# Expert outputs added to rows in device memory as they are made, and a last stage whose down product comes a group later

## The reference

```python
shared = silu(xf @ sg) * (xf @ su) @ sd
masked = expert scores, -1e9 outside the best 4 of 8 groups
top_scores, top_idx = top_k(masked, 4)        # 4 of 32 experts for each token
gates = softmax(top_scores)
pos = place of the token in its expert's list; keep = pos < 1280
buf[e, pos] = xf[token]                       # kept tokens
out_e = (silu(buf @ wg) * (buf @ wu)) @ wd    # 32 experts, hidden 512
contrib = out_e[e, min(pos, 1279)] * gate * keep
out = layernorm(xf + shared + sum of the 4 contribs)
```

## Time and profile before

| | |
|---|---|
| median of 3 timed runs | 2529.51 us |
| profiled execution, time | 2515.5 us |
| its span, first to last instruction | 2514.0 us |
| mean granted TensorE clock | 0.949 |
| PE busy | 2225.7 us, 89% |
| DVE, ACT, POOL busy | 59%, 43%, 51% |
| indirect transfers | 256 scatters, 240 gathers, 256 row fetches |
| moved by DMA | 271.14 MB |

### The profile page before, as it was taken

How to read it: one execution, slowest core, us unless ns; L and a number is a source line. 1 busy time by engine, 2 the same in 40 slices (tenths; PEclk the granted TensorE clock), 3 DMA queues, 4 the chain that set the end, 5 groups by cost and what they waited for, 6 DMA issues and landing times. The chain is left out here.

```text
span 2514.0 us, 45293 instructions
## 1 busy us (share of the span) xinstructions
PE 2225.7 (89%) x12892; PEld 1786.8 (71%) x12892; DVE 1490.4 (59%) x3485; ACT 1076.3 (43%) x2818; POOL 1292.9 (51%) x1564
## 2 busy tenths in 40 slices
PE   6999699999999999506999999999999994887885
PEld 3555366666666666406999999999999994776774
DVE  4666246666666766524555556565655552767766
ACT  3555254454544445204555555555555551222221
POOL 3666211565565564654444444444444444677775
PEclk9999799999999999758999999999999997998997
DMA  4000122233142131104554444444444453344443
GB/s 129 25 0 0 46 77 91 60 78 99 59 98 77 59 117 52 62 1 155 151 154 151 153 158 159 155 155 159 159 159 159 157 154 106 117 130 129 138 127 102
DMA packets 196419, 271.14 MB, mean 108 GB/s; under 512 B 30745, under 2 KB 139057, under 8 KB 196370
## 3 DMA queue, kind: packets, MB, share of 16 engines
q1 hardware_dynamic: 164370, 209.30, 26.4%
q0 software_dynamic: 32000, 61.26, 9.1%
HBM read 182.75 MB, written 87.73 MB: 108 GB/s over the span
## 5 line engine op out<-in xcount | busy, mean ns | idle before, releaser
L1351 POOL DMA_INDIRECT e_xg<-x_rows,e_tok x240 | 243.8, 1016 | 443.2 <-issue 229.2
L967 POOL DMA_INDIRECT slot_token<-tok,a_slot_i x256 | 267.9, 1046 | 214.3 <-issue 95.7
L1636 POOL DMA_INDIRECT f_row<-expert_rows,f_idx x256 | 265.8, 1038 | 89.9 <-issue 76.7
L1479 ACT ACTIVATE e_sg<-e_g 128x448 f32<-128x448 f32 x232 | 126.5, 545 | 420.1 <-PE e_g L1205 420.1
L1529 DVE TENSOR_TENSOR e_hid<-e_sg,e_u 128x448 f32<-128x448 f32 x232 | 144.1, 621 | 246.7 <-PE e_u L1205 242.7
L850 ACT ACTIVATE a_prob<-a_s,a_ntop 128x128 f32<-128x128 f32 x512 | 180.1, 394 | 0.8 <-DVE a_ntop L1147 0.5
L1542 DVE COPY e_out<-e_d 112x512 f32<-112x512 f32 x116 | 80.2, 691 | 150.9 <-PE e_d L1205 150.9
L1205 PE MATMUL e_d<-e_wd1h,e_ht1h 128*112 128x256 f32 x464 | 132.9, 286 | 13.3 <-issue 13.3
L1205 PE MATMUL f_d<-f_wdh,f_hth 128*128 128x256 f32 x256 | 83.0, 324 | 60.3 <-DVE f_htl L1756 60.3
L1727 ACT ACTIVATE f_sg<-f_g 128x512 f32<-128x512 f32 x64 | 38.2, 598 | 224.6 <-PE f_g L1205 224.6
L1205 PE MATMUL e_d<-e_wd0h,e_ht0h 128*112 128x256 f32 x464 | 132.0, 285 | 0.0
(11 more groups left out here) (262 smaller groups left out, 6630.2 us busy)
## 6 DMA issues: line engine op xcount, KB each, us to landing
expert_rows<-a_zero SPq DMA_DIRECT2D x16, 2688.0 KB, 12.6
e_raw_g<-in_eg SPq DMA_DIRECT2D x60, 512.0 KB, 3.4
e_raw_u<-in_eu SPq DMA_DIRECT2D x60, 512.0 KB, 4.4
e_raw_d<-in_ed SPq DMA_DIRECT2D x59, 512.0 KB, 5.9
expert_rows<-e_out SPq DMA_DIRECT2D x58, 448.0 KB, 3.1
x<-in_x SPq DMA_DIRECT2D x16, 512.0 KB, 3.6
x_rows<-x SPq DMA_DIRECT2D x16, 512.0 KB, 3.5
f_xs<-x_rows SPq DMA_DIRECT2D x16, 512.0 KB, 4.9
```

The costliest lines, as they stand in the source:

```text
L967: pool.indirect_dma_start(k.slot_tok, bass.IndirectOffsetOnAxis(ap=slot_i[:, j, q:q + 1], axis=0), k.tok[:, j:j + 1], None, bounds_check=S ...
L1351: pool.indirect_dma_start(xg[a][:, n, :], None, k.x2_d, bass.IndirectOffsetOnAxis(ap=tok[a][:, n:n + 1], axis=0))\
L1479: act.activation(sg[m % 2][:], bank_g[m % 2][:, 0:SETW], ACT.Silu).then_inc(sg_rdy, 1)
L1636: pool.indirect_dma_start(row[a][:, j, q, :], None, k.out_d[0:SLOTS, :], bass.IndirectOffsetOnAxis(ap=idx[a][:, j, q:q + 1], axis=0))\
```

## The change

- Gates and token numbers are scattered together as pairs of 8 bytes. `slot_token` gets two columns; blank slots name rows behind the real ones. The two on-chip tables, and the vector instructions that fill them, are gone, and `place` waits for the scatters of the group before at the gates, five instructions earlier. The zero fill of `expert_rows` is gone; x2 is stored twice, to `x_rows` and to `sum_rows`, in which the sums grow.
- In the expert stage VectorE multiplies the down product by the gates, four instructions for the two copies. GpSimd adds the 448 rows to `sum_rows` by four indirect transfers that add (`add_rows`), two items later. Two items can hold the same token, so the adds of an item wait for those of the item before to land; the wait passes over SyncE, whose `load_dest(w)` (the pairs once more, for the gates and the addresses) waits for the adds of item w-2.
- In the last stage the row fetches and the sixteen adds are gone. SyncE loads x2 for the transposes and the sums for the last addition separately. TensorE makes `down(g-1)` after `turn(g+1)`; the hidden parts have two buffers. VectorE's `summed`, `moments` and `normed` come up to a group later; GpSimd has only `rstd`.
- The plan's last column holds the number of items less one, from which the ends of the loops are worked out; the rounds are the same.

```diff
-                FILLED = SLOTS // NG
-
-                sp.wait_ge(blank_rdy, 1)
-                sp.dma_start(k.slot_tok.rearrange("(p n) a -> p (n a)", p=RT), blank[:]).then_inc(blanked, 16)
+                spare = zero[0:RT, None, :].to_broadcast([RT, TI, D])
+                sp.wait_ge(blank_rdy, 2)
+                sp.dma_start(k.slot_tok.rearrange("(p m n) a -> p m (n a)", p=BLANKS, n=SETW),
+                             blank[:].rearrange("p n a -> p (n a)")[:, None, :]
+                             .to_broadcast([BLANKS, (E * NSET + 1) // BLANKS, 2 * SETW])).then_inc(blanked, 16)
                 sp.wait_ge(zero_rdy, 1)
+                for d in (k.x2_d, k.acc_d):
+                    sp.dma_start(d[B * T:B * T + SETW, :].rearrange("(p n) d -> p n d", n=TI), spare).then_inc(filled, 16)
 
                 def store(g):
-                    sp.dma_start(k.out_d[bass.ds(g * FILLED, FILLED), :].rearrange("(p n) d -> p n d", p=P),
-                                 zero[:, None, :].to_broadcast([P, FILLED // P, D])).then_inc(filled, 16)
                     sp.wait_ge(x2_rdy, ONE + g + 1)
-                    sp.dma_start(k.x2_d[bass.ds(g * GW, GW), :].rearrange("(b t) d -> t b d", b=TG),
-                                 grouped(rows(k.x, g))).then_inc(x2_out, 16)
+                    for d in (k.x2_d, k.acc_d):
+                        sp.dma_start(d[bass.ds(g * GW, GW), :].rearrange("(b t) d -> t b d", b=TG),
+                                     grouped(rows(k.x, g))).then_inc(x2_out, 16)
...
-                                k.tok[:, j:j + 1], None, bounds_check=SLOTS - 1, oob_is_err=False)\
+                                pair[:, j, q, :], None, bounds_check=SLOTS - 1, oob_is_err=False)\
...
+                    dve.wait_ge(tok_rdy, ONE + r)
+                    then(dve.tensor_tensor(pair_gate, ex[:], er[:, :, None].to_broadcast([P, TG, K]), ALU.mult))
...
-                def store(w, a):
+                def load_dest(w, a):
                     start = slots(w)
-                    sp.wait_ge(out_rdy, OUT + NP * (w + 1))
-                    sp.dma_start(k.out_d[bass.ds(start, SETW), :].rearrange("(p n) d -> p n d", n=TI), out[a][:])\
-                        .then_inc(stored[a], 16)
+                    if at_least(w, 2):
+                        sp.wait_ge(added, 16 * TI * (w - 1))
+                        apart(sp, k.past_sp)
+                    sp.dma_start(dest[a][:], k.slot_tok[bass.ds(start, SETW), :].rearrange("(p n) a -> p n a", n=TI))\
+                        .then_inc(dest_in[a], 16)
 
                 def item(w, a):
                     load_tok(w + 2, a)
                     load_up(w + 2, a)
                     load_down(w + 1, 1 - a)
-                    if at_least(w, 1):
-                        store(w - 1, 1 - a)
+                    load_dest(w, a)
...
+                def add_rows(w, a):
+                    pool.wait_ge(out_rdy, OUT + TI * (w + 1))
+                    apart(pool, k.past_pool)
+                    for n in range(TI):
+                        pool.indirect_dma_start(k.acc_d, bass.IndirectOffsetOnAxis(ap=dest[a][:, n, 0:1], axis=0),
+                                                out[a][:, n, :], None, compute_op=ALU.add).then_inc(added, 16)
+
+                def item(w, a, i):
+
+
+                    gather(w + 2, a, i + 1)
+                    if at_least(w, 2):
+                        pool.wait_ge(u_done, ONE + HC * w + 2)
+                        apart(pool, k.past_pool)
+                        pool.wait_ge(dest_in[1 - a], DMA + 16 * (i + a))
+                        apart(pool, k.past_pool)
+                        add_rows(w - 2, a)
+                    down_low(w, a)
...
+                pool.wait_ge(dest_in[1], DMA + 16 * used)
+                apart(pool, k.past_pool)
+                add_rows(last - 1, 0)
+                pool.wait_ge(added, 16 * TI * last)
+                apart(pool, k.past_pool)
+                add_rows(last, 1)
...
-                def copied(w, a, i):
-                    if at_least(i, 1):
-                        dve.wait_ge(stored[a], DMA + 16 * i)
-                    for h in range(NP):
-                        dve.wait_ge(d_done, ONE + NP * w + h + 1)
-                        dve.tensor_copy(out[a][:, 2 * h:2 * h + 2, :],
-                                        bank_d[h][0:RT, :].rearrange("p (t d) -> p t d", t=2)).then_inc(out_rdy, 1)
+                def gated(w, a, i):
+
+                    dve.wait_ge(dest_in[a], DMA + 16 * (i + 1))
+                    gate = dest[a][:].bitcast(F32)
+                    for n in range(TI):
+                        if n % 2 == 0:
+                            dve.wait_ge(d_done, ONE + NP * w + n // 2 + 1)
+                        dve.tensor_scalar(out[a][:, n, :], bank_d[n // 2][0:RT, (n % 2) * D:(n % 2 + 1) * D],
+                                          gate[:, n, 1:2], None, ALU.mult).then_inc(out_rdy, 1)
...
+                def fetch_acc(g, a):
+                    sp.dma_start(acc[a][:], acc_rows[:, bass.ds(g * TG, TG), :]).then_inc(acc_in[a], 16)
...
+                        sp.wait_ge(t_done, ONE + DC * (g + 1))
+                        apart(sp, k.past_sp)
+                        fetch(g + 2, a)
                         sp.wait_ge(sum_rdy, ONE + 2 * (g + 1))
                         apart(sp, k.past_sp)
-                        fetch(g + 2, a)
+                        fetch_acc(g + 2, a)
                         store(g, a)
...
-                    if not first:
-                        pool.wait_ge(row_in[a], 16 * TG * K * i)
-                    pool.tensor_copy(idx[a][:].rearrange("p t q -> p (t q)"),
-                                     k.slot[:, bass.ds(g * TG * K, TG * K)]).then_inc(idx_rdy, 1)
-                    pool.wait_ge(idx_rdy, ONE + g + 1)
-                    apart(pool, k.past_pool)
-                    for j in range(TG):
-                        for q in range(K):
-                            pool.indirect_dma_start(row[a][:, j, q, :], None, k.out_d[0:SLOTS, :],
-                                                    bass.IndirectOffsetOnAxis(ap=idx[a][:, j, q:q + 1], axis=0))\
-                                .then_inc(row_in[a], 16)
+                begin(pool, ve_rdy, rs_rdy)
 
...
+                def group(g, a, i):
+                    up(g)
+                    if not is_last(g):
+                        turn(g + 1, 1 - a, i + a)
+                    if at_least(g, 1):
+                        down(g - 1, 1 - a)
...
+                def summed(g, a, i):
+                    dve.wait_ge(acc_in[a], DMA + 16 * (i + 1))
+                    if at_least(i, 1):
+                        dve.wait_ge(stored[a], DMA + 16 * i)
+                    for h in range(2):
+                        dve.wait_ge(d_done, ONE + 2 * g + h + 1)
+                        dve.tensor_tensor(res[a][:, 2 * h:2 * h + 2, :],
+                                          bank_d[h][:].rearrange("p (t d) -> p t d", t=2),
+                                          acc[a][:, 2 * h:2 * h + 2, :], ALU.add).then_inc(sum_rdy, 1)
...
+                        if m == 0 and at_least(g, 2):
+                            moments(g - 2, a)
+                        if m == 2 and at_least(g, 2):
+                            normed(g - 2, a)
+                    hidden_low(g, a, HC - 1)
+                    if not is_last(g):
                         turned(g + 1)
-                    if finishes:
-                        normed(g - 1, 1 - a)
-                    if not isinstance(i, int) or i:
```

More of the change, by code:

```diff
@@ L41 @@
 FAR = 4 * SLOTS
+BLANKS = max(n for n in range(1, P + 1) if (E * NSET + 1) % n == 0)
 EPS = 1e-5
@@ L1232, in expert_stage @@
         bank_d = [p.bank(f"d{i}") for i in range(2)]
-        g_in, u_in, d_in, tok_in, x_in, stored = ([p.sem(f"{n}{i}") for i in range(2)]
-                                                  for n in ("g_in", "u_in", "d_in", "tok_in", "x_in", "stored"))
+        g_in, u_in, d_in, tok_in, x_in, dest_in = ([p.sem(f"{n}{i}") for i in range(2)]
+                                                   for n in ("g_in", "u_in", "d_in", "tok_in", "x_in", "dest_in"))
+        added = p.sem("added")
         t_done, xh_rdy, xl_rdy = p.sem("t_done"), p.sem("xh"), p.sem("xl")
@@ L1365, in first @@
                     gather(1, 1, 0)
-                    gather(2, 0, 1)
-                    down_low(0, 0)
-                    gather(3, 1, 1)
-                    down_low(1, 1)
+                    item(0, 0, 0)
+                    item(1, 1, 0)
                 def again(i):
-                    gather(2 * i + 2, 0, i + 1)
-                    down_low(2 * i, 0)
-                    gather(2 * i + 3, 1, i + 1)
-                    down_low(2 * i + 1, 1)
+                    item(2 * i, 0, i)
+                    item(2 * i + 1, 1, i)
                 used, last = rounds(pool, first, again)
+                pool.wait_ge(dest_in[1], DMA + 16 * used)
+                apart(pool, k.past_pool)
```

(50 more changed lines are left out.)

214 lines of the change are left out of this document (84 added, 130 removed).

## The result

The changed kernel takes 2659.0 us (median of 4 runs, 2657.1 to 2661.3) where the kernel before takes 2526.9 beside it: ratio 1.052, interval 1.050 to 1.055, 5% slower. The forecast was 2660. Its profiled execution has a span of 2658.4 us and a time of 2660.2. The profiled execution of the kernel before, at 2515.5, lies 11 us under the median of its timed runs; so the medians differ by 132 us where the two traces, on which the readings by stage rest, differ by 144.

The account below looks back on a forecast made before the run. It took TensorE to bound the attention and expert stages and GpSimd the last stage. Attention +1.5, expert +136, border +4.5 and last stage 0 gave +142 us, hence 2660 us, with 8 in 10 between 2570 and 2820.

Parts of the forecast that it names:

- Both waits: Expert stage: load_dest waiting for landed adds, 18.5 us a turn; last stage: turn waiting 6 us a group for its fetch.
- turns: Expert stage: ring of gathers, adds, landing, load_dest and token load, one turn an item, 18.5 us against 16.03.
- Landing: Expert stage: the last add's landing, taken as 4.0 us between 2.28 and 7.5, plus 0.2 to issue load_dest.
- rival 1: Expert stage: adds land in 2.28 us like the quiet scatter, turn 16.8, total 2560 to 2575; chance 0.15.
- Rival 2: Expert stage: dear adds landing in 6.0 to 7.5 us, turn 20.5 to 22.0, total 2770 to 2860; chance 0.22.
- Rival 3: Last stage: fetch not late, gives back 80 to 108 us; expert ring costs 50; total 2485; chance 0.1.
- Expert stage and border: Expert stage +136 us from 56 longer turns, slack and late end; border to the last stage +4.5.
- the slack of 7 us: Expert stage: the token list can be loaded earlier than before, taking about 7 us off.
- the late end: Expert stage: GpSimd's last item ends later, 13.5 us into the item instead of 8.9, adding 4.6 us.
- The border's 30.9: Expert to last stage: GpSimd's empty rounds (13.3 us), then adds of items 56 and 57 in sequence, 30.9 against 26.4.
- Attention stage: Up to the expert stage: +1.5 us from the earlier wait in place(), showing once in the tail; fills and stores 0.
- Last stage: About 0 us, from -25 to +25: the late fetch makes groups 24.6 us in place of GpSimd's 23.5.

Follow-up runs that it names:

- Plain writes: The changed kernel with the expert stage's indirect transfers writing rows instead of adding to them: 2542.5 us in its one run.
- the other order of the fetch: The changed kernel with fetch(g+3) ahead of the sums and the store of group g in the last stage: 2565.8 us, ratio 1.016.
- both orders: The changed kernel with load_dest an item later, behind a token list, and the last stage's fetch ahead of sums and store: 2446.6 us, ratio 0.969.
- the run with late adds: The changed kernel with GpSimd's down_low(w) ahead of the adds instead of behind them: 2858.3 us in its one run.

## Why the prediction was right

It was right in the time, the mechanism and the places. Both waits stand where it put them, and moving each one away took the loss with it. But several of its terms had errors that cancelled, and that 2660 meets 2659.0 so closely is luck: between the two traces it was 144 us for 142 predicted, between the medians 132. Two turns of the trace after, against the steps:

| step of a turn, us | predicted | first | second |
|---|---|---|---|
| first gather to first add | 5.5 | 5.10 | 5.02 |
| first to last add | 4.05 | 5.64 | 5.37 |
| last add to `load_dest` | 4.2 | 3.71 | 4.04 |
| `load_dest` to token list | 2.1 | 1.83 | 1.36 |
| token list to gather | 2.7 | 2.43 | 2.37 |
| sum | 18.5 | 18.7 | 18.2 |

- The add's issue was taken as a gather's, 0.93 us; its median is 1.50. That step was mis-sized by 1.5 us a turn. The four other steps came out 0.2 to 0.7 shorter than predicted and gave it back. A right sum over such errors is partly luck.
- Landing: 4.0 plus 0.2 predicted between bounds of 2.28 and 7.5, 3.7 to 4.0 measured. Rivals 1 and 2 fall by it. Plain writes need 2.8 with SyncE's part, so rival 1's 2.28 plus 0.2 was nearer to the price of a write than of an add. (Its own sum is 43 - 1.4 = 41.6 and, with the attention stage, 43; nothing hangs on it.) Rival 2 was right that an add costs more on GpSimd, but not in the size.
- "TensorE idle by about 2.5 us an item" was not so: between 1500 and 1800 us it is idle for 23.5 us, 1.4 an item. The other 1.0 is in its products, which take longer at the granted clock of 0.96: a product of `e_d` has a mean of 0.301 us in this stretch, and 0.282 in the kernel before.
- Rival 3 wasn't this kernel, but its last stage is what the other order of the fetch gives (308.6 us, 99.6 less than before, in its 80 to 108). Its condition, a fetch issued early in the group, was the right one.
- Expert stage and border: +136 and +4.5 predicted, +142.8 measured together. GpSimd's last subtraction ends at 2223.6; from there to the last stage it is 29.4 us against 26.4, so the border has +3.0 and the stage +139.8. 56 turns of 2.4 and the late end (4.6 predicted, 5.0 measured) make 139, so the slack of 7 us isn't seen.
- The border's 30.9 came near to 29.4 by two errors. The empty rounds were to hold back GpSimd's adds by 13.3 us, as they hold TensorE; GpSimd's next add starts 2.5 us after its last subtraction. And nothing but 0.5 was put behind the last landing, where 8.3 us pass, 7.58 of them in the DRAIN.
- Attention stage: +1.5 predicted, +4.5 measured. The wait in `place` has its 1.5. The rest is there before the first store of x2 (2.2 us at 373 us, 3.0 at the last one), which the prediction put at 0. The seven traces with this same attention stage scatter by nearly as much: the first transposes start between 284.5 and 287.5 us (285.9 before), the sixteen products for the queries behind them take 8.8 to 10.1 us (8.6 before), and the first gather comes between 1140.6 and 1143.3. The one trace of before, at 1137.1, lies below them all, by 3.4 to 6.2. So part of the 4.5 is scatter, and whether something delays the start stays open.
- Last stage: 0 predicted, -2.8 measured. The period was predicted at 24.6 and measured at 24.9; store to fetch 0.9, measured 0.8 and 1.2; landing 4.9, measured 4.1 in the median; the turn 1.5, measured 1.97, at half the granted clock in all of its 13 groups. It is an accident that a wait of nearly the same size took the place of GpSimd's 23.5 us a group.
- Memory traffic fell from 271 to 212 MB. From 400 to 800 us the DMA engines' busy share fell from 0.31 to 0.12 and TensorE's busy time stayed at 390.6 and 390.5 us, so that stretch wasn't bound by it.

## What to carry to other kernels

When a transfer is moved to a queue, write down what stands behind it there and follow it until it comes back: a load of operands behind a wait for results makes a ring, and its turn is all its landings and issues in sequence, even where every engine is half idle. The repair is an order, not less work: what the next item needs goes ahead of every wait for what the last one left (here twice, 116 and 93 us, by moving one load each). The engine and operand in a wait's row are only the last link. To find the cause, make the ring longer or shorter with the same work.

## What the runs showed of the hardware

An indirect transfer that adds to its rows takes GpSimd 1.50 us to issue (median of 232; 112 rows of 1 KB), one that writes them 0.95, a gather 0.94. From the start of the issue to the queue's release behind it there are 3.7 to 4.0 us for an add and 2.8 for a write; half of that difference is the longer issue.

At the end of the expert stage GpSimd's closing DRAIN takes 7.58 us in each of the seven traces of kernels that add, and 9.54 in the kernel before and with plain writes. It delays the next stage only where GpSimd is the last to finish. What sets its length isn't shown.

VectorE is held up when a subtraction of its own falls on GpSimd's and both engines read two tiles in on-chip memory. In the changed kernel, expert stage, VectorE and then GpSimd:

```profile
2202.55 3.59 DVE L1537 TENSOR_TENSOR e_wu0l<-e_raw_u,e_wu0h 128x512 fp32r<-128x512 f32 x1
...
2207.34 0.68 DVE L1537 TENSOR_TENSOR e_wu0l<-e_raw_u,e_wu0h 128x512 fp32r<-128x512 f32 x1
```

```profile
2202.27 3.31 POOL L1366 TENSOR_TENSOR e_wd0l<-e_raw_d,e_wd0h 128x256 fp32r<-128x256 f32 x4
```

The same instruction takes 3.59 us beside GpSimd's four and 0.68 without them. All 56 such subtractions of VectorE that fall on GpSimd's are longer than alone (0.87 to 4.10 us, instead of 0.62 to 0.69). Those into `e_xtl`, which read a bank that TensorE has written, are not: 0.62 us at most for five of them here and for 116 in the kernel before, which has no other kind beside GpSimd's. GpSimd isn't slowed in these rows. Its four start 0.70 us apart as before; the 3.3 us instead of 2.83 come from the first, which starts 0.48 before the add's issue ends, and the same 3.3 are found with both orders. In the run with late adds both engines are slowed at times: GpSimd's four in its 4.17 us start up to 1.24 apart, beside VectorE's at 1.15 to 1.32.

With both orders no such subtraction of VectorE falls on GpSimd's, and none takes over 0.76 us.
